# Edge counting by spans: the table words go into registers during layer 0's query projection, and one feature round stands ahead of each of 20 spans

## What is computed

```python
def _L0_gnn_ref(h, src, dst, W, attn_l, attn_r, W_res):
    ft = jnp.einsum('nhd,od->nho', hv, W)
    a1 = jnp.sum(ft * attn_l, axis=-1)
    a2 = jnp.sum(ft * attn_r, axis=-1)
    e = leaky_relu(a1[src] + a2[dst])
    w = exp(e - segment_max(e, dst)[dst])
    alpha = w / segment_sum(w, dst)[dst]
    agg = segment_sum(alpha[:, :, None] * ft[src], dst)
    return relu((agg + res).reshape(n, H * DOUT))
```

## Time and profile before

| what | us |
|---|---|
| median of 3 runs (1996.58 to 1996.91) | 1996.63 |
| the profiled execution, its own time | 2001.18 |
| its span, from the first to the last instruction | 1999.4 |
| PE busy in the span | 1821.5 |
| DVE busy | 720.9 |
| ACT busy | 392.3 |
| DVE busy on L1701, the 125x128 one-hot, x207 | 51.6 |
| PE busy on L826, the counting product, x207 | 90.0 |

### The profile page before, as it was taken

One profiled execution on the slowest core, in us unless ns is written; L12 is line 12 of the kernel. 1 busy time (PEld: TensorE's weight loads), 2 busy tenths in 40 slices (PEclk: granted clock), 3 DMA queues, 4 the chain that ended last, 5 costly groups with the idle time before them and its releaser, 6 DMA issues.

```text
span 1999.4 us, 24143 instructions
## 1 busy us (share of the span) xinstructions
PE 1821.5 (91%) x7984; PEld 1105.2 (55%) x7985; DVE 720.9 (36%) x1792; ACT 392.3 (20%) x1030; POOL 131.7 (7%) x170
## 2 busy tenths in 40 slices
PE   7999999876699998599997999999999999699994
PEld 4555566333233344366665965555579579555562
DVE  4212222554688989601114401141111124522121
ACT  2431210123111222211112422000221211212120
POOL 0000000000000000111113100000000000022221
PEclk9999999976599999799998999999999999799897
DMA  6004000000000111544564310010010013545565
GB/s 185 0 1 155 14 1 0 31 1 1 1 31 31 46 32 39 197 141 154 186 222 140 99 49 25 23 48 0 1 48 1 0 63 93 204 115 145 159 187 124
DMA packets 53755, 149.56 MB, mean 75 GB/s; under 512 B 9394, under 2 KB 20038, under 8 KB 53157
## 3 DMA queue, kind: packets, MB, share of 16 engines
q1 hardware_dynamic: 34101, 88.97, 12.8%
q0 software_dynamic: 12032, 37.59, 7.5%
q10 hardware_dynamic: 7536, 21.85, 3.1%
HBM read 117.92 MB, written 37.83 MB: 78 GB/s over the span
## 4 chain that ended last, share of the span: by engine, by line
PE 80%; DVE 9%; DVEq 3%; DMA 3%; issue 3%; ACT 0%; POOL 0%; ACTq 0%; SPq 0%; POOLq 0%
PE PS L686 23%; PE PS L1001 10%; PE PS L696 8%; PE PS L1111 4%; PE PS L1042 4%; PE PS L1131 4%; PE PS L757 4%; PE PS L1083 4%; DVE WRA L1752 3%; PE PS L1069 3%; PE PS L826 2%; PE PS L910 2%; DMA WS<-in_fW 2%; PE PS L919 2%; DVE WRB L1752 2%
## 5 line engine op out<-in xcount | busy, mean ns | idle before, releaser
L686 PE MATMUL PS<-WS,XT 128*125 128x384 f32 x960 | 313.2, 488 | 1.4 <-issue 1.4
L686 PEld LDWEIGHTS PS<-WS,XT 128*125 128x125 f32 x960 | 180.3, 189 | 129.3 <-issue 3.3
L1001 PE MATMUL PS<-WS,XGT 128*128 x600 | 199.6, 490 | 0.0
L1001 PEld LDWEIGHTS PS<-WS,XGT 128*128 128x128 f32 x600 | 113.2, 192 | 74.5 <-issue 2.2
L696 PE MATMUL PS<-XT,WS 128*128 128x416 f32 (+1 forms) x432 | 151.2, 512 | 0.0
L1752 DVE SCALAR_TENSOR_TENSOR WRA<-RB,U,AT 125x500 f32<-125x500 f32 (+1 forms) x240 | 140.0, 646 | 4.6 <-PE PS L919 2.0
L1886 DVE TENSOR_TENSOR YS<-PS,EBB 128x768 f32<-128x768 f32 x48 | 46.0, 958 | 244.7 <-PE PS L1001 191.5
L826 PE MATMUL PS<-OHK,OHS 125*128 125x500 bf16 x207 | 90.0, 510 | 39.5 <-DVE OHK L1703 37.3
L696 PEld LDWEIGHTS PS<-XT,WS 128*128 128x128 f32 x432 | 81.6, 189 | 69.2 <-issue 69.2
L1111 PE MATMUL PS<-WS,XGT 128*128 x288 | 104.7, 516 | 10.8 <-DMA WS<-in_fW 9.7
L910 PE MATMUL PS<-WRA,F 125*64 125x500 f32 (+1 forms) x480 | 101.4, 541 | 10.0 <-DVE WRA L1752 9.1
(11 more groups left out here) (312 smaller groups left out, 2093.0 us busy)
## 6 DMA issues: line engine op xcount, KB each, us to landing
WS<-in_ewT SPq DMA_DIRECT2D x8, 2304.0 KB, 10.6
WS<-in_fW SPq DMA_DIRECT2D x16, 1152.0 KB, 8.3
WS<-in_w SPq DMA_DIRECT2D x5, 2304.0 KB, 10.3
expert_rows<-YS ACTq DMA_DIRECT2D x25, 384.0 KB, 2.3
xn_rows<-XN ACTq DMA_DIRECT2D x20, 336.0 KB
RB<-expert_rows SPq DMA_DIRECT2D x12, 488.3 KB
WS<-in_wp SPq DMA_DIRECT2D x2, 2304.0 KB, 11.3
WS<-in_W SPq DMA_DIRECT2D x2, 2304.0 KB, 8.6
```

The costliest lines, as they stand in the source:

```text
L686: last = nc.tensor.matmul(ps[0:T, 0:HC], lhsT[:, k, t * T:(t + 1) * T], w[:, k, b * HC:(b + 1) * HC], start=(k == 0), stop=(k == KC - 1))
L1001: last = nc.tensor.matmul(PS[:, 4 + 2 * a + b, 0:HC], XGT[:, a, k, :], WS[:, bass.ds(slot, 1), k * C + b * HC:k * C + (b + 1) * HC].rearra ...
```

## The change

It has three parts.

**Registers.** The 25 loads of `n` on TensorE move from the spans into the query projection: job r is followed by the load for span r, and for r below 7 also by that of span r + 18. TensorE's wait for `table_ready` moves ahead of the projection's first job. The running sum `done_before` is no longer loaded: both engines add up the turns in a register (`snap`). On VectorE one word takes the place of three: `256 * n + t0` is loaded behind the job's `QT` write, with the same order of spans, and unpacked ahead of the span by a mask and a shift. Fifty registers, 25 on each engine, now hold a value from the projection to the span.

**Table.** Beside node tile 3 VectorE no longer scans for the running sum; it packs the word with one instruction.

**Rounds.** `FT_AT` goes. One round stands ahead of each of the spans 0 to 19, on TensorE and on ScalarE.

```diff
--- before.py
+++ after.py
@@ -49,7 +49,6 @@
 SLOTS = 3
 TURNS = -(-ET // SLOTS)
 ETP = TURNS * SLOTS
-FT_AT = {2 * t: t for t in range(NT)}
 WSLOTS = 6
 DEN_AT = {3: (1, 3), 7: (5, 7), 9: (9,)}
 RSLOTS = 3
@@ -750,6 +749,8 @@
         ps = begin(J.at["att_max"])
         nc.tensor.matmul(ps[:, 0:1], sel44, gmax[:, 4:5], start=True, stop=True).then_inc(pe_filled, 1)
         w = weights(2)
+        pe.wait_ge(table_ready, 1)
+        turns_of = {}
         for q in range(KC):
             for c, (o, n) in enumerate(CH):
                 ps = begin(J.at[f"q0_{q}"] + c)
@@ -757,6 +758,8 @@
                     last = nc.tensor.matmul(ps[:, 0:n], w[:, k, q * P:(q + 1) * P], XT[:, k, o:o + n],
                                             start=(k == 0), stop=(k == KC - 1))
                 last.then_inc(pe_filled, 1)
+                for v in range(3 * q + c, NW, 18):
+                    turns_of[v] = nc.tensor.value_load(table[0:1, 1, v:v + 1], min_val=2, max_val=TURNS)
             if q == 1:
                 pe.wait_ge(arw_ready, 1)
                 ps = begin(J.at["att_cols"])
@@ -797,7 +800,6 @@
                 projected(t - 1)
         projected(NT - 1)
 
-        pe.wait_ge(table_ready, 1)
         pe.wait_ge(iota_done, 1)
         m = J.at[f"proj0_{NT - 1}"] + 1
         pe.wait_ge(act_emptied, J.emptied("act", m))
@@ -816,8 +818,8 @@
             last.then_inc(tr_filled, 1)
 
         for w in range(NW):
-            n = nc.tensor.value_load(table[0:1, 1, w:w + 1], min_val=2, max_val=TURNS)
-            done_before = nc.tensor.value_load(table[0:1, 2, w:w + 1], min_val=0, max_val=TURNS * NW)
+            n = turns_of[w]
+            done_before = nc.tensor.snap(done_before + turns_of[w - 1]) if w else 0
             ps = PS[:, w % WB, 0:KW]
 
             def counted(u, first):
@@ -826,9 +828,8 @@
                     nc.tensor.matmul(ps, OHS[:, k, :], OHK[:, k, :], start=(first and k == 0), stop=True,
                                      skip_group_check=True).then_inc(oh_free, 1)
 
-            if w in FT_AT:
-                for q in range(2):
-                    turn_round(2 * FT_AT[w] + q)
+            if w < len(TRR):
+                turn_round(w)
             if w >= WB:
                 pe.wait_ge(at_ready, w - WB + 1)
             counted(done_before, True)
@@ -1233,9 +1234,8 @@
         act.wait_ge(iota_done, 1)
         nc.scalar.activation(F[:, :, :, D:D + 1], P2.unsqueeze(3), ACT.Copy).then_inc(f_ready, 1)
         for w in range(NW):
-            if w in FT_AT:
-                for q in range(2):
-                    empty_round(2 * FT_AT[w] + q)
+            if w < len(TRR):
+                empty_round(w)
             act.wait_ge(acc_done, w + 1)
             nc.scalar.activation(AT[:, :, w * WD:(w + 1) * WD], PS[0:T, w % WB, 0:KW].rearrange("p (d s) -> p s d", s=NT),
                                  ACT.Copy).then_inc(at_ready, 1)
@@ -1587,12 +1587,11 @@
                 V.tensor_scalar(span[:, 3, :], span[:, 6, :], -MAGIC, None, ALU.add)
                 V.drain()
                 V.tensor_scalar(span[:, 6, :], span[:, 3, :], float(-SLOTS), float(ETP), ALU.mult, ALU.add)
-                V.memset(span[:, 5, :], 0.0)
                 V.drain()
                 V.tensor_tensor(span[:, 2, :], span[:, 2, :], span[:, 6, :], ALU.min)
-                V.tensor_tensor_scan(out=span[:, 4, :], data0=span[:, 3, :], data1=span[:, 5, :], initial=0.0, op0=ALU.add, op1=ALU.add)
-                V.drain()
-                V.tensor_tensor(span[:, 4, :], span[:, 4, :], span[:, 3, :], ALU.subtract)
+                V.drain()
+                V.scalar_tensor_tensor(out=span[:, 4, :], in0=span[:, 3, :], scalar=256.0, in1=span[:, 2, :], op0=ALU.mult,
+                                       op1=ALU.add)
                 V.drain()
                 V.tensor_copy(table, span[:, 2:5, :])
                 V.drain().then_inc(table_ready, 1)
@@ -1636,6 +1635,7 @@
         V.tensor_scalar(ARW[0:H, :], ARW[0:H, :], gcol[0:H, :], None, ALU.subtract)
         V.tensor_scalar(ARW[32:32 + H, :], ARW[32:32 + H, :], gcol[32:32 + H, :], 0.0, ALU.add, ALU.max)
         V.drain().then_inc(arw_ready, 1)
+        window = {}
         for r in range(18):
             o, n = CH[r % 3]
             if r == 9:
@@ -1645,6 +1645,8 @@
             dve.wait_ge(qexp, r + 1)
             V.scalar_tensor_tensor(out=QT[:, r // 3, o:o + n], in0=ps[:, 0:n], scalar=0.0, in1=TQ[:, r % 4 // 2, r % 2, 0:n],
                                    op0=ALU.max, op1=ALU.add).then_inc(dve_emptied, 1)
+            for w in range(r, NW, 18):
+                window[w] = nc.vector.value_load(table[0:1, 2, w:w + 1], min_val=2 * 256, max_val=TURNS * 256 + 255)
         V.drain()
 
         def normal_rows(t):
@@ -1687,9 +1689,8 @@
         V.memset(zeros, 0.0)
         V.drain().then_inc(iota_done, 1)
         for w in range(NW):
-            t0 = nc.vector.value_load(table[0:1, 0, w:w + 1], min_val=0, max_val=ETP - SLOTS)
-            n = nc.vector.value_load(table[0:1, 1, w:w + 1], min_val=2, max_val=TURNS)
-            done_before = nc.vector.value_load(table[0:1, 2, w:w + 1], min_val=0, max_val=TURNS * NW)
+            done_before = nc.vector.snap(done_before + n) if w else 0
+            t0, n = nc.vector.snap(window[w] & 255), nc.vector.snap(window[w] >> 8)
             if w == 0:
                 nc.vector.engine_nop().then_inc(oh_free, SLOTS)
             with nc.vector.Fori(0, n) as j:
```

## The result

The changed kernel is slower: 2009.72 us in the median of 6 runs (2004.35 to 2010.49), against 1996.61 before (6 runs, 1990.13 to 1999.71). The ratio is 1.0066, with an interval of 1.0041 to 1.009. The forecast was 1947.6 us, so 62 us are missing.

What follows compares the result with a forecast made beforehand. Nothing bound the counting all the time; register loads between spans and feature rounds let VectorE idle. Gains of 38.6 + 1.95 + 7.9 + 0.6 (tail) = 49.0 us gave 1947.6 us, range 1940 to 1964.

Steps and rivals of the forecast that it cites:

- What replaces the loads. Three snaps: VectorE's span boundary in the counting: sum, mask and shift replace three loads of 1.86 us, at 0.25 us.
- the dear end: VectorE's span boundary: three snaps cost up to 0.74 us; as a rival 1959.4 us, chance 0.08.
- the rival of registers that do not hold: Fifty long-lived values: each written back and read again at its span; 2003.7 us, chance 0.02.
- A boundary without loads: VectorE between spans, last OHS to next OHS: 0.86 us against 2.47, or 0.61 without loads or snaps.
- the term of 38.6: Gain at VectorE's span boundaries in the counting: 24 boundaries x (1.86 - 0.25) = 38.6 us.
- The entry: Start of the counting stage: three loads of 2.2 us go, less 0.25 for snaps, a gain of 1.95 us.
- The rounds: Feature rounds, one a span: 6.9 us lost against 14.8, gain 7.9; per-span loss 0.1 at 2.4 GHz, 1.08 at 1.2.
- The level of the clock: TensorE's clock in the counting: upper level mostly, one span in four at the lower; above 0.8 expected.
- all upper: Rival for the counting: clock stays at 2.4 GHz through all spans, 53.9 us gained, 1942.7 us; chance 0.25.
- The moved loads at nothing: TensorE's 25 loads in the query projection are covered by its products: 0 us, with 15.5 kept as a case.
- TensorE's loads alone give nothing but delay the rounds: Span boundaries: TensorE's loads run beside VectorE's and are shorter in sum, gaining nothing alone, but delay the rounds.
- What would show it wrong: Signs: VectorE idle on L826 over 10 us, L814 at 2.92 us, idle before L757, or loads left between spans.

Runs made afterwards that it cites:

- e1_sum_ahead: Changed kernel with VectorE's first turn of each span written out ahead of the loop; 1941.2 us, ratio 0.9717.
- e2_rounds_only: Kernel before with one feature round ahead of each of spans 0 to 19 and nothing else; 1985.74 us, ratio 0.9941.
- e6_tensor_registers_only: Kernel before with spread rounds, TensorE's loads in the projection and its sum in a register, VectorE's loads kept; 1981.56 us, ratio 0.9923.
- e7_tensor_loads_in_spans: e1_sum_ahead with TensorE's number of turns loaded ahead of each span, none in the query projection; 1959.44 us, ratio 0.9804.
- e8_moved_loads_doubled: e1_sum_ahead with each load in the query projection made twice on both engines; 1941.91 us, ratio 0.9722.

## Why the prediction was wrong

**The step that failed** is "What replaces the loads. Three snaps". It priced the sum, the mask and the shift once for each boundary, at 0.25 us, with 0.74 as the dear end, and took from the diff's text that one operation is asked for. The program has none of them ahead of the loop. VectorE's sum is worked out where it is first used, inside the loop, and from all earlier words each time. The range of that term was wrong in kind: it had a size for each boundary and none for each turn, growing with the span. The nearest thing in my list, the rival of registers that do not hold, gave 2003.7 us, but by another way: the words do hold (e1_sum_ahead keeps 25 on each engine and has no load in the counting), the sum is what isn't held. Its time came near by chance. In the trace of the changed kernel the durations of the 164 operations add up to 39.9 us, and the 58 grown ones at the loop's head take 16.9 us, 13 more than at 63 ns each. That is 53 of the 64.9 us between this kernel's closing (541.3) and e1_sum_ahead's (476.4). How the other 12 are shared between the gaps from one operation to the next, the written-out turn and the lower clock of the thinned stage was not measured.

Point by point, with the sum repaired:

- *A boundary without loads*: forecast 0.86 us, measured 0.60 in most spans of e1_sum_ahead, which is the 0.61 that I had derived without any snap. Executed ahead, the sum is one operation of 0.17 us and runs under the last OHK. All 24 boundaries take 15.2 us in place of 60.4: the term of 38.6 should have been 45.2.
- *The entry*: first OHS forecast near 371.4, in the changed kernel at 371.57, after 0.56 us of idling against 2.72. TensorE's first round starts at 371.09. This held (in e1_sum_ahead the idling is 0.39 us, and the start at 372.82 since the stage ahead ended later):

```profile
371.09 0.92 PE L816 MATMUL PS<-WBD,XT 128*125 128x128 f32 x6 [0.93 <-DVEq L1690]
...
371.57 0.26 DVE L1702 TENSOR_SCALAR OHS<-io,ES 125x128 bf16<-125x128 bf16 x1 [0.56 <-DVEq L1695]
```

- *The rounds*: a two-turn span with a round takes 2.46 us from first to last OHS in e1_sum_ahead (mean of spans 8 to 19), 0.16 over the free 2.30. I had 0.1 at the upper clock; the mixed value was 0.35. But the written-out turn lowers the free value to 2.11 (spans 20 and 24), and over that the loss is 0.35. Over all spans the time from first to last OHS falls by 13.9 us, where I had 7.9; a part of this is the written-out turn. The gain of spreading alone, 0 to 8 us expected, is 12 by the medians of e2_rounds_only and 8.4 by the closing of the counting.
- *The level of the clock*: right where the gaps are closed. 0.97 in e1_sum_ahead, so the "all upper" case. In the changed kernel the gaps opened again late, and the clock went to 0.50 there.
- *The moved loads at nothing*: right. From the first start to the last, the projection's products take 76.7 us before, after, and with twice the loads:

```profile
L757 PE MATMUL PS<-XT,WS x216: 510/512/618, 193.3 to 269.9; 128*128 128x416 f32 x72, 128*128 128x418 f32 x36
```

```profile
L758 PE MATMUL PS<-XT,WS x216: 510/512/618, 193.6 to 270.3; 128*128 128x416 f32 x72, 128*128 128x418 f32 x36
```

- *TensorE's loads alone give nothing but delay the rounds*: right beside VectorE's loads (5.1 us in e6_tensor_registers_only), 12.2 us without them (e7_tensor_loads_in_spans).
- *The sum*: 49.0 us forecast; with the in-loop additions out, 59.9 us in the counting by the traces (536.3 to 476.4) and 56 by the medians.
- *What would show it wrong*: I had named VectorE's idling on L826 over 10 us. It came true, and it misled: 34.6 us are put down to TensorE, which had been done for 1.13 us on average.

**What stays open.** The counting explains 5.0 us of the loss. The medians differ by 13.1 (by 8 to 18 with the interval), the spans of the two profiled runs by 6.8. In these TensorE's wait for the second layer's expert weights differs as well, 9.7 us before and 14.6 after, with the idle time in all:

```profile
L1111 PE MATMUL PS<-WS,XGT 128*128 x288 | 104.7, 516 | 10.8 <-DMA WS<-in_fW 9.7 <-ACTq L1315 1.1
```

```profile
L1112 PE MATMUL PS<-WS,XGT 128*128 x288 | 107.9, 529 | 15.8 <-DMA WS<-in_fW 14.6 <-ACTq L1315 1.1
```

That wait is 5.1 to 17.8 us over the ten traces, with no order by the length of the counting. Whether the changed kernel falls into the longer waits more often was not tried.

## What to carry to other kernels

A value that is named once in the source is not for that held once: look in the program's order of instructions at where its arithmetic stands, above all when its first use is inside a loop, and give it a use ahead of the loop. A chain of such values costs more with every step, so compare the first pass of a stage with the last one, not only the totals. When a wait of one engine disappears, a load of another engine that was beside it becomes the next price: move both or expect little.

## What the runs showed of the hardware

VectorE's sequencer takes some 0.3 us for each fused register operation of this kind (seven start within 537.0 to 538.8 us in the changed kernel), and the engine idles meanwhile (2.41 us there) if they stand ahead of a wait inside the loop. One short operation is not seen: with the sum of 0.17 us ahead of the loop in e1_sum_ahead, a boundary measures 0.60 us, no more than the 0.61 of loop work that I had derived. TensorE's register loads of 0.30 us, 50 of them among the projection's products in e8_moved_loads_doubled, lengthened these by less than 0.1 us in 76.7. TensorE's granted clock was 0.97 in the counting of e1_sum_ahead, where it had been 0.69 before with 0.50 in its last 25 us. The Trainium skill (TensorE: Matmul & The Clock Gate, What's actually happening) says that activity releases the throttle; the traces agree, as the level rose where the gaps closed.
